# Reordering the splits of K, of x and of the results in a batched graph-attention kernel on one core

## What is computed

```
z_l = h @ W_lang.T ;  z_g = h @ W_grav.T ;  v = h @ W_V.T
zn  = z_l / max(norm(z_l), EPS)
A_l = max(zn @ zn.T, 0) * not_eye
A_g = exp(-max(sq + sq.T - 2 * z_g @ z_g.T, 0) / (2 sigma^2)) * not_eye
K   = w_l * rownorm(A_l * mask) + (1 - w_l) * rownorm(A_g * mask)
x   = layernorm(x + (K @ v) @ W_O.T)
```

## Time and profile before

| | |
|---|---|
| median of 3 runs | 997.1 us (996.71 to 997.12) |
| the profiled execution | 998.76 us, of which the span of its instructions is 997.0 us |
| TensorE matmuls busy | 965.2 us, 97% of the span |
| VectorE busy | 702.8 us, 70% |
| ScalarE busy | 323.7 us, 32% |
| GpSimd (POOL) busy | 151.9 us, 15% |
| share of the 16 DMA engines | 37.7% on the main queue |
| TensorE's granted clock | 0.998 of full speed |

### The profile page before, as it was taken

One profiled execution on the slowest core, in us unless ns is written; L12 is line 12 of the kernel. 1 busy time (PEld: TensorE's weight loads), 2 busy tenths in 40 slices (PEclk: granted clock), 3 DMA queues, 4 the chain that ended last, 5 costly groups with the idle time before them and its releaser, 6 DMA issues.

```text
span 997.0 us, 13226 instructions
## 1 busy us (share of the span) xinstructions
PE 965.2 (97%) x4802; PEld 825.5 (83%) x4802; DVE 702.8 (70%) x1954; ACT 323.7 (32%) x632; POOL 151.9 (15%) x155
## 2 busy tenths in 40 slices
PE   9999999999999999999999999999999999999997
PEld 7788887888878888787888879888788888879885
DVE  4557757767776677767777677677757777676488
ACT  4333243232432424233232432424233232432331
POOL 0202111021200212111021200212002121200231
PEclk9999999999999999999999999999999999999999
DMA  8323253442534524253432524425344342623001
GB/s 221 75 48 82 95 140 102 117 142 75 133 95 112 153 82 120 96 130 123 112 127 85 143 90 111 157 79 123 96 119 135 101 124 93 148 85 127 1 22 64
DMA packets 215873, 106.78 MB, mean 107 GB/s; under 512 B 140545, under 2 KB 187649, under 8 KB 215809
## 3 DMA queue, kind: packets, MB, share of 16 engines
q1 hardware_dynamic: 213696, 104.90, 37.7%
q10 hardware_dynamic: 2112, 1.05, 0.4%
HBM read 63.44 MB, written 42.47 MB: 106 GB/s over the span
## 4 chain that ended last, share of the span: by engine, by line
PE 79%; DVE 13%; issue 3%; DMA 2%; ACT 2%; SPq 0%; POOLq 0%; POOL 0%; DVEq 0%
PE ring L326 19%; PE ring L327 18%; PE ring L328 18%; PE g_bank L326 8%; PE g_bank L328 8%; PE g_bank L327 8%; DVE whole L742 2%; DVE bn L951 2%; DVE y L944 2%; DVE xT_lo L746 2%; DMA off_turned<-off 1%; DVE kT_lo L926 1%; DMA off<-off_turned 1%; ACT kT_hi L609 1%; DVE u_odd_lo L732 1%
## 5 line engine op out<-in xcount | busy, mean ns | idle before, releaser
L732 DVE TENSOR_TENSOR zg_lo<-ring,zg_hi 128x512 fp32r<-128x512 f32 x64 | 43.9, 690 | 107.3 <-ACT zg_hi L568 107.3
L1152 POOL TENSOR_TENSOR rstd<-var_eps,neg_half 128x1 f32<-128x1 f32 x64 | 46.0, 719 | 440.4 <-DVE var_eps L959 440.4
L326 PE MATMUL ring<-xT_hi,wgT_hi 128*128 128x512 f32 x256 | 101.8, 398 | 0.1
L326 PE MATMUL ring<-xT_hi,wlT_hi 128*128 128x512 f32 x256 | 101.1, 395 | 0.0
L327 PE MATMUL ring<-xT_lo,wgT_hi 128*128 128x512 f32 x256 | 100.1, 391 | 0.0
L328 PE MATMUL ring<-xT_hi,wgT_lo 128*128 128x512 f32 x256 | 99.8, 390 | 0.0
L328 PE MATMUL ring<-xT_hi,wlT_lo 128*128 128x512 f32 x256 | 99.7, 389 | 0.0
L327 PE MATMUL ring<-xT_lo,wlT_hi 128*128 128x512 f32 x256 | 99.7, 389 | 0.0
L326 PE MATMUL ring<-wvo_hi,xT_hi 128*128 128x512 f32 x256 | 99.7, 389 | 0.0
L328 PE MATMUL ring<-wvo_hi,xT_lo 128*128 128x512 f32 x256 | 99.6, 389 | 0.0
L327 PE MATMUL ring<-wvo_lo,xT_hi 128*128 128x512 f32 x256 | 99.6, 389 | 0.0
(11 more groups left out here) (126 smaller groups left out, 2226.8 us busy)
## 6 DMA issues: line engine op xcount, KB each, us to landing
xb<-in_x_dram SPq DMA_DIRECT2D x60, 256.0 KB, 4.5
out_dram<-y SPq DMA_DIRECT2D x60, 256.0 KB, 2.0
k_turned<-ag SPq DMA_DIRECT2D x56, 256.0 KB, 2.2
al<-k_turned SPq DMA_DIRECT2D x224, 64.0 KB, 2.0
y<-in_x_dram SPq DMA_DIRECT2D x14, 1024.0 KB, 5.4
off_turned<-off SPq DMA_DIRECT2D x28, 384.0 KB, 2.3
off<-off_turned SPq DMA_DIRECT2D x112, 96.0 KB, 2.2
y<-in_x_dram SPq DMA_DIRECT2D x4, 256.0 KB, 5.5
```

The costliest lines, as they stand in the source:

```text
L326: nc.tensor.matmul(psum, lh, rh, start=k == 0, stop=False)
L732: nc.vector.tensor_tensor(pair[1][:, i, :], bank[:, :], pair[0][:, i, :].bitcast(F32), ALU.subtract).then_inc(evacuated, 1)
L1152: nc.gpsimd.tensor_tensor(rstd[:, i:i + 1], var_eps[:, i:i + 1], neg_half[:, 0:1], ALU.pow)\
```

## The change

In the last third of `batch` alone, the order of work on ScalarE and VectorE changes. ScalarE makes the high parts of all four blocks of K and then those of the four blocks of x, where it alternated between them. VectorE turns the first two blocks of x before it makes the low part of block 0 of K, then makes the low parts of u 2 and u 3 and of blocks 1 to 3 of K, and only then begins with x and the results; the steps of these are interleaved in a new order. `last_two`, the prologue and the programs of the other three engines are as before. The first hunk is ScalarE's, the second VectorE's.

```diff
@@ -677,11 +677,10 @@
                     s.hi("u", 1, i, u[1 - parity])
                 s.hi_k(0)
                 s.hi("u", 1, 3, u[1 - parity])
-                s.hi_k(1)
+                for i in range(1, T):
+                    s.hi_k(i)
                 for k in range(T):
                     whole_hi_part(b + 2, k, xT)
-                    if k + 2 < T:
-                        s.hi_k(k + 2)
 
             def last_two(b, stream):
                 s = Steps(b, stream)
@@ -1004,22 +1003,34 @@
                 s.turn_k(3)
                 s.lo("u", 1, 0, u_next)
                 s.lo("u", 1, 1, u_next)
+                x_transpose(b + 2, 0)
+                x_transpose(b + 2, 1)
                 s.lo_k(0)
                 s.lo("u", 1, 2, u_next)
-                s.lo_k(1)
-                x_transpose(b + 2, 0)
                 s.lo("u", 1, 3, u_next)
-                for i in range(T):
-                    if i + 1 < T:
-                        x_transpose(b + 2, i + 1)
-                    whole_lo_part(b + 2, i, xT)
-                    s.residual(0, i)
-                    s.row_sums(0, i)
-                    if i + 2 < T:
-                        s.lo_k(i + 2)
-                    s.statistics(0, i)
-                    if i:
-                        s.normalise(0, i - 1)
+                for i in range(1, T):
+                    s.lo_k(i)
+                whole_lo_part(b + 2, 0, xT)
+                s.residual(0, 0)
+                x_transpose(b + 2, 2)
+                s.row_sums(0, 0)
+                whole_lo_part(b + 2, 1, xT)
+                s.statistics(0, 0)
+                x_transpose(b + 2, 3)
+                s.residual(0, 1)
+                s.normalise(0, 0)
+                s.row_sums(0, 1)
+                whole_lo_part(b + 2, 2, xT)
+                s.statistics(0, 1)
+                whole_lo_part(b + 2, 3, xT)
+                s.residual(0, 2)
+                s.normalise(0, 1)
+                s.row_sums(0, 2)
+                s.statistics(0, 2)
+                s.residual(0, 3)
+                s.normalise(0, 2)
+                s.row_sums(0, 3)
+                s.statistics(0, 3)
                 s.normalise(0, T - 1)
 
             def last_two(b, stream):
```

## The result

The changed kernel takes 972.55 us (median of 4 runs, 971.08 to 975.67) against 996.9 us before (4 runs, 996.04 to 997.12), a ratio of 0.9756 with a 95% interval of 0.9728 to 0.9784. The forecast was 974.5 us with a range of 970.5 to 981. The profiled execution took 975.67 us with a span of 973.9 us, so its span is 23.1 us shorter than that of before.

A forecast was written before the change was run, and what follows sets the result against it. TensorE was taken to bound the kernel, losing 1.83 us per batch to waits for VectorE's low parts of K. 998.76 - 25.6 + 3.0 = 976.2 us profiled; the same 22.6 us off the median 997.1 gives 974.5 us, range 970.5 to 981.

The forecast's parts named there:

- Removed waits: TensorE's two waits per batch for low parts of K (blocks 2, 3) go: 1.83 us x 14 = 25.6 us.
- Turns in the gap, and the low part of u 3 ahead of block 1, at nothing: On VectorE, two turns of x fit a 2.54 us gap and block 1 keeps 0.45 us spare: no cost.
- Block 3's load: ScalarE's copy of block 3 of K waits a little for its load; TensorE keeps over 2 us to spare.
- The tail: VectorE's work after block 3: first diagonal 1.23 us sooner, last ties with TensorE (0.04 us spare); another 0.58 us free.
- The rival in which the tail binds: VectorE's tail 0.6 to 1.6 us later makes TensorE wait in 13 batches; at 1.0 us, 980 us; chance 0.14.
- Late transfers: Late loads of K and turned Gram blocks give back 3.0 us: 1.7 in one batch, 0.8 in two, 0.5 elsewhere.
- Load: Rival: turned Gram blocks meet the last result's store every batch, arriving 2.1 us later; 20 us back, 995 us; chance 0.04.
- Slower: Rival: block 3's load holds ScalarE's copies of x, the tail and TensorE; at 2.8 us delay 1002 us; chance 0.04.

The follow-up runs named there:

- the kernel with K ahead alone: Against the kernel before: blocks 1 to 3 of K ahead on ScalarE and VectorE, turns of x behind them, rest in old loop; 990.38 us, ratio 0.9936.

## Why the prediction was right

- *Removed waits.* 1.83 us x 14 = 25.6 us were forecast. The stretch is 10.88 us instead of 12.70, 1.82 us less, in the batch shown, and as short in all 14. Right.
- *Turns in the gap, and the low part of u 3 ahead of block 1, at nothing.* Block 0's low part starts 1.37 us before the first result matmul, as before; block 1 at 1.43 us after it instead of 1.35, and TensorE does not wait. Right.
- *Block 3's load.* ScalarE starts block 3 at 1.99 us after the first result matmul in this batch; 2.10 was worked out. In the other batches the wait for the load is longer, 0.7 us in the mean of all 14.
- *The tail.* This term was mis-sized, and a second error hid it. First diagonal in the batch shown, worked out: 16.45 us after the first result matmul; measured: 15.87. About 0.5 of these 0.6 us are the two places where a normalise waits for POOL's root: row sums to normalise took 1.81 us (643.59 to 645.40) and 1.82 us (645.87 to 647.69), where the row of before that I took had 2.06 (the last section). But this batch has the shortest wait for block 3's load. Over the 13 batches that run into a next one of the loop the first diagonal comes at 15.87 to 17.29 us, at 16.34 in the mean, since the loads of an ordinary batch hold the tail longer than the one row that stood for them. That the mean lies so near the 16.45 is luck. The 0.63 us of room at the last diagonal belong to the batch shown; in five of the 13 there is next to none. The rival in which the tail binds fell because only one batch, the fourth, was clearly as late as it needs, 0.6 us past the 16.45.
- *Late transfers.* 3.0 us were to come back. In the profiled executions 25.6 - 23.1 = 2.5 us did, by the medians 25.6 - 24.4 = 1.2 us. The sum was nearly right and its parts were not: the waits for the exponent grew by 0.9 us, to 3.8 instead of the 5 to 7 forecast, and half-rate matmuls after the longest of them, which the prediction did not have, cost some 1.5 us. In the fourth batch 1.7 us were to be paid in full; the wait grew from 1.41 to 2.08 us, because the room at the last diagonal took up most of the rest. That the parts add up is luck.
- *Load.* That the turned blocks would be late in every batch because the last result's store is near did not come: ten of 13 batches show no wait for the exponent in the changed kernel's trace. SyncE's queue in the fourth batch and in the sixth:

```profile
297.38 0.33 SPq L241 DMA_DIRECT2D out_dram<-y  x1
299.34 0.33 SPq L266 DMA_DIRECT2D off_turned<-off  x1
303.76 1.75 SPq L269 DMA_DIRECT2D off<-off_turned  x4
```

```profile
416.97 0.33 SPq L241 DMA_DIRECT2D out_dram<-y  x1
418.93 0.33 SPq L266 DMA_DIRECT2D off_turned<-off  x1
421.24 1.76 SPq L269 DMA_DIRECT2D off<-off_turned  x4
```

The loads can go only when the store has landed. In both batches the store of the turned blocks is issued 1.96 us behind the result's; in one the loads follow 4.42 us later, in the other 2.31 us. So the distance from the result's store does not decide. The Trainium skill (DMA: Bandwidth & Descriptors, Latency and other measured facts) says that the access to HBM takes ten times as long under high load. No run here shows that load made the late stores late.
- *Slower.* ScalarE's wait for block 3 is there 15 times, but 9.3 us together and 1.4 us at most at a time (1.5 us in the fourth batch, in two waits); it would have had to be 2.4.

What makes some transfers late is open. In the traces of both kernels they stand in the same batches (the fourth, the seventh and the eleventh of the loop). In the fourth and the eleventh it is the store of the turned Gram blocks: it lands 4.40 and 4.14 us after its issue in the changed kernel's trace, 4.43 and 4.30 us before, 2.3 us in the median, and about 2.9 us in four of the eight experiments' traces. Nothing was tried on it.

## What to carry to other kernels

When one engine is full and still waits at a fixed place, ask first which queue the late operand stood in, and what in front of it nobody was waiting for: two instructions moved into an idle stretch gave two thirds of the gain here. Then follow the moved work to its next deadline: putting the urgent first pushes the rest back, and the same order of K with the turns behind it kept only 6 of the 24 us. Room can be measured: add an instruction of known length where it is suspected, twice, and see at which length the time, and the number of waits, begins to rise. And look at every batch before one stands for all: the one shown here had the shortest wait of its kind.

## What the runs showed of the hardware

**After a wait of 2 us TensorE's clock fell.** In the late batch of the changed kernel's trace, TensorE:

```profile
308.47 0.45 PE L326 MATMUL g_bank<-zl_hi 128*128 128x384 f32 x1 [2.08 <-DVE ag L834]
308.75 0.34 PE L327 MATMUL g_bank<-zl_lo,zl_hi 128*128 128x384 f32 x1
...
310.08 0.53 PE L328 MATMUL g_bank<-zl_hi,zl_lo 128*128 128x384 f32 x1
310.40 0.53 PE L326 MATMUL g_bank<-zl_hi 128*128 128x384 f32 x1
```

and the busy times by stretch (engines' busy time and instructions, then TensorE's granted clock, share of DMA, GB/s):

```profile
301.00:308.00 7.00, 5.39 (x24) 4.13 (x22) 2.59 (x12) 1.70 (x5) 0.00 (x0) 1.00 0.41 91
310.00:313.50 3.50, 3.50 (x13) 3.50 (x13) 3.46 (x11) 1.50 (x3) 0.00 (x0) 0.54 0.98 154
```

After the wait of 2.08 us matmuls of 384 columns start 0.17 to 0.18 us apart for a while, then, from 310.08, 0.32 us apart, with a granted clock of 0.54 in that stretch: that is the level of 1.2 GHz instead of 2.4. Ten matmuls later it is full again; 10 x 0.15 = 1.5 us. The wait of 1.41 us in the same batch before was followed by none of this. In the kernel with K ahead alone, waits of 2.94 and 2.57 us were followed by 18 and 11 such matmuls. In the ten traces all seven waits for the exponent of 1.93 us or more had such matmuls behind them, and none of those up to 1.78 us. The length of the wait does not decide alone, though. In the prologue TensorE waits some 2 us in every trace, and the clock fell after that in five of the ten. Two executions of the changed kernel differ in it; a row of the timeline and, below it, the busy times of the stretch that follows:

```profile
32.75 0.47 PE L326 MATMUL ring<-kT_hi,u_odd_hi 128*128 128x512 f32 x1 [1.98 <-DVE kT_lo L745]
33.40:36.70 3.30, 3.30 (x10) 2.56 (x9) 1.54 (x5) 0.00 (x0) 0.00 (x0) 0.50 1.02 160
```

```profile
32.37 0.47 PE L326 MATMUL ring<-kT_hi,u_odd_hi 128*128 128x512 f32 x1 [2.02 <-DVE kT_lo L745]
33.00:36.70 3.70, 3.70 (x18) 3.08 (x17) 2.26 (x6) 0.60 (x1) 0.00 (x0) 1.00 1.14 179
```

So in the late batch a wait that grew from 1.4 to 2.1 us cost more than the difference, and what the executions of one kernel differ by is seen in this clock too: the changed kernel's four runs had a mean of 0.995, 0.996, 0.998 and 0.999, and took 975.67, 973.58, 971.51 and 971.08 us.

**POOL's root depends on what VectorE does beside it.** Before, in the batch of the earlier trace rows, a normalise of VectorE and the root of POOL that began under it, the one behind the 2.06 us:

```profile
662.60 0.54 DVE L963 TENSOR_SCALAR y<-y,mv,rstd 128x512 f32<-128x512 f32 x1
```

```profile
662.76 0.78 POOL L1152 TENSOR_TENSOR rstd<-var_eps,neg_half 128x1 f32<-128x1 f32 x1 [2.09 <-DVE var_eps L959]
```

and in the changed kernel three roots of POOL, the first of them under the low part of a block of x:

```profile
642.10 0.92 POOL L1163 TENSOR_TENSOR rstd<-var_eps,neg_half 128x1 f32<-128x1 f32 x1 [2.58 <-DVE var_eps L958]
644.83 0.54 POOL L1163 TENSOR_TENSOR rstd<-var_eps,neg_half 128x1 f32<-128x1 f32 x1 [1.81 <-DVE var_eps L958]
647.11 0.55 POOL L1163 TENSOR_TENSOR rstd<-var_eps,neg_half 128x1 f32<-128x1 f32 x1 [1.74 <-DVE var_eps L958]
```

```profile
641.94 0.68 DVE L745 TENSOR_TENSOR xT_lo<-whole,xT_hi 128x512 fp32r<-128x512 f32 x1
```

The same instruction on 128x1 elements took 0.78 us under a normalise, 0.92 us under a low part of x, and 0.55 us with VectorE idle, at 647.11. Under a turn of x, or an addition that reads PSUM, it was 0.54 us too (638.98 and 644.83). This holds for every batch: the 42 roots of the results in the loop of before that began under a normalise took 0.77 or 0.78 us, the 14 of the changed kernel under a low part of x 0.92 or 0.93 us, and all of them ended 0.40 us after the VectorE instruction did, whether they had run beside it for 0.38 or for 0.52 us. The Trainium skill (SBUF — State Buffer, SBUF: two separate sides) says that VectorE and GpSimd lock one pair of ports between them, and that a VectorE instruction in a two-port mode, or one with two inputs in SBUF, takes it for its whole length when it starts first. The rows of the low part of x, which has two inputs in SBUF, agree, and so do those of the addition, which has one; in which mode the normalise ran no row shows, and that it was this lock was not tried by an experiment. In the changed kernel the normalise of one row tile no longer directly follows the variance of the next, so the root runs beside other work, and that is where the 0.24 us per root of the tail came from.
